# A fused three-stage kernel: the side work of its attention stage is laid out by round

## The reference

```python
x = x + 0.5 * ffn(layernorm(x))      # 8 experts, threshold routing with a capacity of 1024 tokens each
x = x + attention(layernorm(x))
x = x + 0.5 * ffn(layernorm(x))
# attention, 16 heads of width 16, K = 4 "nodes" per head:
q, k, v, logits = x @ Wq, x @ Wk, x @ Wv, x @ Wr
node_probs   = softmax(logits)                       # over the 4 nodes
expected_pos = cumsum(node_probs over tokens) - node_probs
cos, sin     = RoPE tables interpolated at expected_pos, then summed over nodes with node_probs
q_r, k_r     = q * cos + rotate_half(q) * sin, k * cos + rotate_half(k) * sin
scores       = q_r @ k_r.T / 4 + log(node_probs @ node_probs.T + 1e-8), causal
out          = softmax(scores) @ v @ Wo
```

## Time and profile before

| | us |
|---|---|
| median of three runs | 2907.16 |
| the profiled execution | 2896.46 |
| its span | 2894.6 |
| TensorE (PE) busy | 2448.1 (85%) |
| VectorE (DVE) busy | 1711.7 (59%) |
| ScalarE (ACT) busy | 1702.9 (59%) |
| GpSimd (POOL) busy | 997.9 (34%) |
| first to last exponential of the units | 536.0 to 2528.7 |

### The profile page before, as it was taken

One profiled execution on the slowest core, in us unless ns is written; L12 is line 12 of the kernel. 1 busy time (PEld: TensorE's weight loads), 2 busy tenths in 40 slices (PEclk: granted clock), 3 DMA queues, 4 the chain that ended last, 5 costly groups with the idle time before them and its releaser, 6 DMA issues. The chain is left out here.

```text
span 2894.6 us, 104325 instructions
## 1 busy us (share of the span) xinstructions
PE 2448.1 (85%) x45990; PEld 1896.7 (66%) x45990; DVE 1711.7 (59%) x3627; ACT 1702.9 (59%) x2174; POOL 997.9 (34%) x1497
## 2 busy tenths in 40 slices
PE   7298444587899999899999989999999999973885
PEld 4165222466788887778888777888877888841553
DVE  7732278788576567866566786666676111167431
ACT  6222123456677777667777766777776777662221
POOL 1188700334222224423222442222244222110787
PEclk9699776799999999999999999999999999986997
DMA  6555401221212112212111221211122111162565
GB/s 233 160 103 101 78 18 30 60 53 47 60 57 56 48 46 79 66 49 59 55 53 52 79 66 53 58 53 53 54 74 69 44 47 49 42 204 72 105 102 74
DMA packets 185109, 207.28 MB, mean 72 GB/s; under 512 B 35984, under 2 KB 151712, under 8 KB 184480
## 3 DMA queue, kind: packets, MB, share of 16 engines
q1 hardware_dynamic: 158880, 165.60, 19.3%
q0 software_dynamic: 24576, 34.10, 7.6%
q10 hardware_dynamic: 1152, 0.26, 0.0%
HBM read 131.68 MB, written 76.02 MB: 72 GB/s over the span
## 5 line engine op out<-in xcount | busy, mean ns | idle before, releaser
L1697 PEld LDWEIGHTS at_mix<-at_val,at_ew 128*64 128x64 f32 x34816 | 1223.7, 138 | 241.3 <-issue 36.0
L1281 ACT ACTIVATE at_ew<-at_ring 128x1024 f32<-128x1024 f32 (+1 forms) x1280 | 1124.7, 898 | 364.4 <-PE at_ring L1679 358.2
L1697 PE MATMUL at_mix<-at_val,at_ew 128*64 128x68 f32 x34816 | 1263.0, 224 | 44.7 <-DVE at_mixed L1543 28.7
L1679 PE MATMUL at_ring<-at_qT,at_kT 98*64 98x512 bf16 (+3 forms) x5120 | 698.9, 353 | 57.9 <-ACT at_ew L1281 35.8
L1202 POOL TENSOR_SCALAR_AFFINE_SELECT at_ew<-at_ew 128x256 f32<-128x256 f32 x512 | 294.3, 579 | 1074.2 <-ACT at_ew L1281 1073.5
L1543 DVE TENSOR_TENSOR at_mixed<-at_mix,at_prob 128x272 f32<-128x272 f32 x256 | 112.3, 439 | 440.4 <-PE at_mix L1697 439.1
L1679 PEld LDWEIGHTS at_ring<-at_qT,at_kT 98*64 98x64 bf16 x5120 | 228.5, 112 | 111.4 <-ACT at_ew L1281 47.6
L1224 POOL TENSOR_TENSOR at_val<-at_vo,at_val 128x256 f32<-128x256 f32 x384 | 267.4, 717 | 7.5
L344 POOL DMA_INDIRECT out_dram<-ffn_xn,ffn_idx_all x128 | 210.0, 1641 | 43.4 <-issue 35.0
L334 POOL DMA_INDIRECT ffn_xn<-table,ffn_idx_all x128 | 126.2, 986 | 278.4 <-DMA ffn_idx_all<-ffn_idx_hi 240.3
L1762 PE MATMUL at_side<-at_w_all,at_turned 128*64 128x512 f32 (+1 forms) x1024 | 197.8, 531 | 13.8 <-DVE at_bounded L1536 5.2
(11 more groups left out here) (243 smaller groups left out, 2727.1 us busy)
## 6 DMA issues: line engine op xcount, KB each, us to landing
table<-ffn_xn SPq DMA_DIRECT2D x32, 512.0 KB, 6.3
q_parts<-at_parts SPq DMA_DIRECT2D x64, 192.0 KB, 2.5
k_parts<-at_parts SPq DMA_DIRECT2D x64, 192.0 KB, 3.0
at_qT<-q_parts SPq DMA_DIRECT2D x128, 96.0 KB
at_kT<-k_parts SPq DMA_DIRECT2D x64, 192.0 KB
ffn_front<-in_L_attn_x_dram SPq DMA_DIRECT2D x16, 512.0 KB, 5.3
ffn_w_in<-in_L_ffn_w_dram SPq DMA_DIRECT2D x32, 256.0 KB, 3.6
at_xin<-out_dram SPq DMA_DIRECT2D x32, 256.0 KB, 6.0
```

The source lines that it names most:

```text
L1281: act.activation(ew[u % NE_BUF][:, a:b], ring[u % 2][:, a:b], ACT.Exp).then_inc(s["exp_ready"], 1)
L1679: lastm = pe.matmul(ring[u % 2][h:h + HALF, at:at + (CH - t) * P], kT[q][:, kc + j * P + h:kc + j * P + h + HALF], qT[q][:, qc + t * P:qc ...
L1697: m = pe.matmul(mix[block_of[u] % 2][h:h + HALF, t * K * VW:(t + 1) * K * VW], ew[u % NE_BUF][:, col + h:col + h + HALF], val[q][:, tile0 ...
```

## The change

The turns are laid out round by round. Round 0 keeps its four turns of 24 units. Every later first round (96 units) becomes one turn (`WIDE`), every second round (224 units) seven turns of 32 (`MID`). Each kind has its own places on every engine. The stretch in which weighted products come one unit earlier is now six units long: places 22 to 27 of a `MID` turn, 69 to 74 of a `WIDE` one. VectorE's steps are cut into smaller ones (the two rotations apart, the positions in four steps, products and sums in four pieces of 1024 columns in place of two of 2048 outside round 0). In round 0 a few places move by one, and the reciprocal root's two instructions on ScalarE (`next_rsqrt`) go from place 20 to 16, ahead of `trig`. Last, TensorE turns the rotated q and k with 8 instructions in transpose mode over 128 columns of weights in place of 16 products with the identity over 64.

```diff
-    SHORT, LONG = 24, 40
-    N_SHORT = 4
+    SHORT, MID, WIDE = 0, 1, 2
+    N_SHORT, N_MID = 4, 7
...
-    turns, at = [], 0
-    while at < U:
-        m = len(turns)
-        turns.append((at, SHORT if m < N_SHORT else LONG))
-        at += turns[-1][1]
+    rounds = [first_unit[v] for v in range(V) if v == 0 or visits[v][1] != visits[v - 1][1]] + [U]
+    turns = []
+    for r in range(len(rounds) - 1):
+        size = rounds[r + 1] - rounds[r]
+        count, kind = (N_SHORT, SHORT) if r == 0 else (N_MID, MID) if r % 2 else (1, WIDE)
+        turns += [(rounds[r] + n * (size // count), size // count, kind) for n in range(count)]
+        assert size % count == 0
     posts, free = {}, 0
...
+    STORE_AT = (20, 22, 53)
...
-        BURST = 26
+        BURST = (None, 22, 69)
...
-                    if at == (10 if short else 14) and new is not None:
+                    if at == (10, 12, 28)[kind] and new is not None:
...
-                SHORT_AT = (3, 6, None, 8, 9, 12, 15, 18, 16, 23, 20)
-                LONG_AT = (4, 6, 10, 8, 16, 18, 20, 23, BURST + 2, BURST + 4, BURST + 3)
-
-                def unit(u, at, short, new, fin, post):
-                    where = SHORT_AT if short else LONG_AT
+                SHORT_AT = (3, 6, None, 8, 9, 12, 15, 19, 17, 23, 16)
+                MID_AT = (4, 6, 9, 8, 14, 16, 18, 21, 24, 28, 22)
+                WIDE_AT = (6, 12, 18, 17, 36, 38, 44, 52, 71, 68, 55)
+
...
-                def node_products(t):
+                def node_products(t, c, n):
                     dve.wait_ge(s["trig_ready"], t + 1)
                     if t > 0:
                         dve.wait_ge(s["qkT_ps"], t)
-                    for n, w in ((0, probabilities(t)), (2, g_t[:, :])):
-                        ch.add(dve.tensor_tensor(prods[:, n:n + 2, :].rearrange("p c (f n) -> p (c f) n", n=NK),
-                                                 cs[:, :, :].rearrange("p c (f n) -> p (c f) n", n=NK),
-                                                 w.unsqueeze(1).to_broadcast([P, 2 * NF, NK]), ALU.mult))
-
-                def node_sums(n):
+                    w = (probabilities(t) if c < 2 else g_t[:, :]).unsqueeze(1).to_broadcast([P, n * NF, NK])
+                    ch.add(dve.tensor_tensor(prods[:, c:c + n, :].rearrange("p c (f n) -> p (c f) n", n=NK),
+                                             cs[:, c % 2:c % 2 + n, :].rearrange("p c (f n) -> p (c f) n", n=NK), w, ALU.mult))
+
+                def node_sums(c, n):
                     ch.wait()
-                    ch(dve.tensor_reduce(sums[:, n:n + 2, :].rearrange("p c n -> p (c n)"),
-                                         prods[:, n:n + 2, :].rearrange("p c (n k) -> p (c n) k", k=K), AX.X, ALU.add))
+                    ch(dve.tensor_reduce(sums[:, c:c + n, :].rearrange("p c n -> p (c n)"),
+                                         prods[:, c:c + n, :].rearrange("p c (n k) -> p (c n) k", k=K), AX.X, ALU.add))
...
-                SHORT_AT = (0, 1, 6, 8, None, 10, 12, 13, 14, 18, 19, 20, 21, 23)
-                LONG_AT = (1, 2, 5, 8, 10, 14, 17, 20, 22, 30, 32, 25, 34, 33)
...
+                AT = {"weights": (1, 1, 2), "rotate": (2, 2, 4), "rotate_2": (2, 3, 6), "join": (3, 4, 8), "squares": (14, 18, 44),
+                      "bound": (20, 23, 58), "residual": (None, 9, 22), "shift": (6, 5, 14), "softmax": (8, 8, 18),
+                      "positions": (10, 12, 28), "whole": (10, 12, 29), "first_angles": (11, 13, 31), "count_turns": (12, 14, 33),
+                      "angles": (13, 15, 36), "absolute": (13, 16, 38), "statistics": (15, 17, 41), "normalise": (23, 24, 60)}
+                PRODUCTS_AT = ({18: 0, 21: 2}, {26: 0, 28: 1, 29: 2, 31: 3}, {75: 0, 79: 1, 83: 2, 87: 3})
+                SUMS_AT = ({19: 0, 22: 2}, {27: 0, 29: 1, 30: 2, 31: 3}, {77: 0, 81: 1, 85: 2, 89: 3})
...
-                                    for h in range(0, P, HALF):
-                                        at = (g * 4 + n) * P + h
-                                        lastm = pe.matmul(side[h:h + HALF, n * GP + g * P:n * GP + (g + 1) * P],
-                                                          qkr[:, at:at + HALF], ident[:, :],
-                                                          start=(n % 2 == 0 and g == 0), stop=False, skip_group_check=True)
+                                    at = (g * 4 + n) * P
+                                    lastm = pe.matmul(side[:, n * GP + g * P:n * GP + (g + 1) * P], qkr[:, at:at + P], ident[:, :],
+                                                      is_transpose=True, start=(n % 2 == 0 and g == 0), stop=False, skip_group_check=True)
...
-                LONG_AT = (1, 3, 7, 9, 13, 15, 17, 20, 24, BURST)
+                MID_AT = (1, 3, 6, 8, 11, 13, 15, 18, 22, 24)
+                WIDE_AT = (2, 8, 14, 20, 26, 34, 40, 48, 56, 64)
...
-                    if not short and (at == 0 or at >= BURST):
+                    if kind != SHORT and BURST[kind] <= at <= BURST[kind] + 5:
                         weigh_until(u)
...
```

130 lines of the change are left out of this document (79 added, 51 removed).

## The result

The changed kernel takes 2953.51 us (median of 4 runs, 2947.41 to 2957.76), the kernel before in the same comparison 2907.72: a ratio of 1.0152, 95% interval 1.0125 to 1.0178. It is 1.5% slower. The forecast said 2936, in a range of 2870 to 2975. The profiled execution took 2957.76 us with a span of 2955.9, 61.3 more than before. Of these, 50.6 lie between the first exponential and the end of round 7. Another 3.3 lie ahead of that stretch and 7.4 behind it. These two no trace gives a cause for: over the thirteen profiles of this case the first exponential starts at 531.4 to 539.3 us and what follows the last one takes 362 to 373, and kernels with the same code there differ as much. So the forecast's +28.6 stands against +50.6 in these rounds, and against +45.8 between the medians.

The account below looks back on a forecast made before the run. It took odd rounds to last as long as TensorE's instructions, any TensorE wait there adding in full. 36.9 - 104.3 + 63 + 25 + 8 = +28.6 on 2907.2 gave 2936 us, range 2870 to 2975.

Parts of the forecast that it names:

- transposes, a time: TensorE turning rotated q and k by transpose mode: saves 0.7 us a time, between nothing and 1.9.
- work moved to rounds 1, 3, 5, 7: These rounds get more prepared pairs (10.6 us of TensorE each) or posts (2.35 us each): together +36.9 us.
- rounds 2, 4, 6: Even rounds lose prepared pairs, posts and most of their waits and half clock: -104.3 us.
- trig idle: Turns of 32: TensorE's scores wait for an exponential behind trig on ScalarE, 3.0 us a turn, 63 us in all.
- half clock behind it: TensorE's granted clock falls after two in three trig waits, 1.7 us lost each: 1.2 a turn, 25 us in all.
- VectorE's queue at the turn's start: VectorE's smaller pieces in odd rounds, put at nothing; 25 us if the slack covering them were gone.
- round 0: Reciprocal root, ahead of trig, waits for VectorE's variance; TensorE waits longer and half clock lengthens: +8 us (0 to +16).
- Rival 4: Even rounds' waits come from blocks, not side work: +16 us, forecast's case 2952 us; no own chance, widens the others.
- Rival 2: Turns of 32: trig's wait does not show, ScalarE's lead or the six-unit stretch covering it; -59.4, 2848 us, chance 0.16.
- Rivals 1 and 3: Clock behind trig's waits: holds (+3.6, 2911 us, chance 0.20) or falls long each time (+75, 2982 us, chance 0.12).
- rival 3: Clock falls long after each trig wait, as in round 0: 21 x 2.2 us more, 2982 us, chance 0.12.
- At nothing: Costed at zero: VectorE's smaller pieces in odd rounds (25 us if cover were gone), SP's stores and loads, the lead's transposes.

Follow-up runs that it names:

- experiment 2: Kernel before, with only the rotated queries and keys turned by 8 transposes instead of 32 products: 2881.25 us, ratio 0.9946.
- experiment 8: Changed kernel with project_qk ahead of the scores in turns of 32 and VectorE's join moved from place 4 to 6: 2856.85 us, ratio 0.9858.
- experiment 1: Changed kernel with project_qk ahead of the scores of its place on TensorE in turns of 32: 2876.25 us, ratio 0.9929.
- experiment 11: Kernel with all repairs together, with VectorE's node products and sums in turns of 96 whole, not halved: 2849.25 us, ratio 0.9801.
- experiment 4: Kernel before, with trig alone moved two places forward in the long turns, to the place of project_qk: 2991.72 us, ratio 1.0325.

## Why the prediction was right, and which sizes were off

The direction, the mechanism that decides and the sign of each term held. The terms, forecast against measured (differences of rounds; the last column says by what):

| Term | forecast | measured | from |
|---|---|---|---|
| transposes, a time | -0.7 | -0.6 to -0.8 | experiment 2, by rounds and by rows |
| work moved to rounds 1, 3, 5, 7 | +36.9 | +49.1 | experiment 8 against before |
| rounds 2, 4, 6 | -104.3 | -102.3 | the windows after |
| trig idle | 63 | 48 | 21 waits of 2.29 |
| half clock behind it | 25 | 18.6 | TensorE's busy time, experiment 1 against after |
| VectorE's queue at the turn's start | 0 | +21.3 | experiment 8 against 1 |
| round 0 | +8 | +15.7 | the windows after |

Experiment 1 puts idle time and clock together at 66.8 us: 48.2 less idle and 18.6 less busy in the three rounds. Nine half-rate stretches of 3.4 us account for 15 of the 18.6; the rest is not explained. The last six rows sum to +50.6 with the 66.8 (the transposes are contained in the work of the rounds); the forecast's were +28.6. The median came 17 us above the forecast. That it came so near is in part luck: trig with its clock was 21 too dear, and the stall left out is 21, so the two largest misses cancel.

*Work moved.* 12 us too low. A post was priced at 2.35 us from its own matmuls; in round 7, which prepares nothing, one post more came with 4.1 us (294.0 - 289.9). Its own rows grew by 2.5, so 1.6 us belongs to its surroundings and stays open. Three posts make 5 us of the 12. Before, rounds 1, 3 and 5 held the projections of 5.5 pairs and not of 5.6, 3 us in all. And experiment 8 still leaves TensorE idle for 5.7 us in these rounds, 4.8 more than before.

*Even rounds.* Round 2 was to keep about 6 us of waits and keeps 5.5. What is left is not mostly a trig wait, as the text said, but one load of k from memory (1.8 us), two places with no releaser (1.9) and 1.3 behind an exponential. Rival 4 is out; which of the forecast's reasons thinned the round is open but for the halved pieces, which did not (experiment 11).

*Trig.* Rival 2 had named ScalarE's lead or the six-unit stretch as cover. Neither covered it. The 3.0 us a turn came to 2.29, because TensorE's own work in the sum was too small. From the product at 1306.69 to its idle time at 1311.87 it worked 5.18 us, where the sum had 4.64 and 0.13 (the last product runs its full 1.12 and not the 0.94 between two starts, and the two behind the first take 1.05 and 1.00); with two diagonal products it was 4.47 and not 3.94 and 0.13. So the first turn, with ScalarE late by the forecast's 0.4, waited 7.44 - 5.18 = 2.26, and those with two diagonal products 2.56 or 2.25 and not 3.1. The 0.4 was right where it came, but it came in 6 turns of 21. Experiment 4 met the 3.0 us exactly, in turns of 40.

*The clock.* Rivals 1 and 3 bracketed it: it fell behind 9 of 21 waits, not behind 14, for 3.4 us each time. (Two thirds of 1.7 are 1.13 a turn, which makes 24 and not 25.) The upper bound was read too high: of the 6.7 us at half rate at the 4.01 us wait TensorE was busy 4.42, for the stretch began at 665.5, 2.3 us before the wait ended. Experiment 4 shows rival 3's case, 0.7 us of waiting away. The Trainium skill ("TensorE: Matmul & The Clock Gate", section "Why this matters for your kernels") warns of idle gaps between bursts; these traces agree, but the gaps that it names are longer than the 1.9 to 2.6 us that already cost something here, and the measurement decides.

*Round 0.* The step of about 2.1 us longer a turn, less 0.7, and 2.4 for the clock gave +8, half of what it was. The wait for `var` came as foretold (23.7 us in four turns), but ended in two idle times of 5.54 and 2.01 us in place of one of 4.01, 3.5 us a turn more, and the clock went from 0.91 to 0.86.

*At nothing.* This step failed: "VectorE's smaller pieces in odd rounds" had been costed at nothing, with 25 us if the cover were gone. The averages had room (33 + 7.5 of 56 us), but the turn's start does not: the last products stand at places 28 to 31, rotation and join follow at 2 to 4, and the shift at 5 has ScalarE's exponentials behind it. A sum over a turn does not show a queue at one place of it.

## What to carry to other kernels

When a step that holds an engine for long (here two table loads and two sines, 4.7 us) moves, look at what the engine that waits has in its own queue *ahead* of the instruction that will wait, not at how much work it has in the turn: the same 3.6 us of matmuls hide the step or don't, depending on which side of one scores instruction they stand. A gap costs more than its length once the clock falls behind it, and steeply: a mean of 2.3 us of idle cost 3.2 in the changed kernel, and 3.0 cost 5.1 in experiment 4. And where a list of waits gives one releaser, follow it one step further for the longest of each kind; here one line hid two causes, with repairs worth 65 and 21 us.
